# Macaron layer on one core: attention operands transposed by DMA, context normalised on three engines, steps reordered

## What is computed

```python
x = x + 0.5 * ffn(layernorm(x))
x = x + attention(layernorm(x))
x = x + 0.5 * ffn(layernorm(x))
# ffn: W = base + mean|w - base| * sign(w - base); (silu(x W1') * (x W3')) W2', inner width 1792
# attention: 32 query heads of 16, 8 key/value heads (4 queries each), rotary embedding,
# scores / 16, causal mask over 1024 tokens, softmax, context, dense projection with bias
```

## Time and profile before

| | |
|---|---|
| median of three runs | 1528.28 us |
| the profiled execution, its own time | 1528.74 us |
| its span, first to last instruction | 1527.0 us |
| busy: TensorE, VectorE, ScalarE, GpSimd | 1452.4, 869.9, 646.4, 158.5 us |
| granted TensorE clock, mean | 0.98 |
| last projection matmul ends | 572.2 us |
| last parts_k written (L1273), wd_raw load issued (L393) | 579.33, 579.36 us |
| first score matmul of attention | 581.54 us |
| four context transpositions (L1751), start of the first to end of the last | 0.63 to 0.66 us |

### The profile page before, as it was taken

One profiled execution on the slowest core, in us unless ns is written; L12 is line 12 of the kernel. 1 busy time (PEld: TensorE's weight loads), 2 busy tenths in 40 slices (PEclk: granted clock), 3 DMA queues, 4 the chain that ended last, 5 costly groups with the idle time before them and its releaser, 6 DMA issues.

```text
span 1527.0 us, 25186 instructions
## 1 busy us (share of the span) xinstructions
PE 1452.4 (95%) x9648; PEld 650.4 (43%) x9648; DVE 869.9 (57%) x1362; ACT 646.4 (42%) x900; POOL 158.5 (10%) x235
## 2 busy tenths in 40 slices
PE   1999999999999995999999999999999999999998
PEld 0444444444444452343434343334444444444443
DVE  7998414414453767899999999955412412412212
ACT  5863112212222454688888888763212112112111
POOL 1000000000000441223232222210000000000000
PEclk9999999999999995799999999999999999999999
DMA  9605500000000001000000000024000000000000
GB/s 387 221 0 192 232 0 1 0 0 1 1 1 1 1 1 35 2 2 2 2 23 10 3 2 3 2 97 193 1 0 0 29 0 0 28 0 1 28 0 27
DMA packets 17035, 58.42 MB, mean 38 GB/s; under 512 B 4912, under 2 KB 4912, under 8 KB 16432
## 3 DMA queue, kind: packets, MB, share of 16 engines
q1 hardware_dynamic: 16944, 57.15, 9.7%
HBM read 40.63 MB, written 15.20 MB: 37 GB/s over the span
## 4 chain that ended last, share of the span: by engine, by line
PE 92%; DVE 4%; issue 1%; ACT 1%; DMA 1%; POOL 0%; SPq 0%; DVEq 0%; ACTq 0%; POOLq 0%
PE ps L1482 38%; PE ps L1503 17%; PE ps L1741 10%; PE ps L1656 7%; PE ps L1722 5%; PE ps L1643 4%; PE ps L1845 3%; PE ps L1529 2%; PE ps L1476 1%; PE ps L1751 1%; DVE rowmax L1310 1%; PE ps L1615 1%; PE ps L1660 1%; DMA w_raw<-w1t 1%; PE ps L1618 1%
## 5 line engine op out<-in xcount | busy, mean ns | idle before, releaser
L778 ACT ACTIVATE probs<-ps 128x1024 f32<-128x1024 f32 (+3 forms) x384 | 296.1, 814 | 64.6 <-PE ps L1722 61.5
L1482 PE MATMUL ps<-xt_hi,w_all 128*128 128x512 f16 x896 | 275.9, 381 | 9.3 <-DVE w_all L989 9.3
L1310 DVE TENSOR_REDUCE rowmax<-ps 128x2 f32<-128x1024 f32 (+3 forms) x208 | 237.1, 1140 | 15.8 <-PE ps L1664 7.3
L1144 DVE SCALAR_TENSOR_TENSOR hb<-ps,scal,silub 128x512 f32<-128x512 f32 x56 | 42.0, 750 | 267.4 <-PE ps L1482 267.4
L1656 PE MATMUL ps<-ka,qa 48*128 48x512 f16 (+3 forms) x768 | 165.8, 346 | 16.4 <-DVE rowmax L1310 10.1
L1482 PE MATMUL ps<-xt_lo,w_all 128*128 128x512 f16 x448 | 170.8, 381 | 0.0
L1741 PE MATMUL ps<-probs,vs 128*32 128x512 f32 (+3 forms) x1536 | 164.4, 500 | 0.0
L1314 DVE TENSOR_REDUCE rowmax<-ps 128x1 f32<-128x512 f32 x192 | 131.1, 683 | 16.9 <-PE ps L1656 14.0
L1482 PEld LDWEIGHTS ps<-xt_hi,w_all 128*128 128x128 f16 (+1 forms) x896 | 87.9, 98 | 115.4 <-issue 11.7
L1722 PE MATMUL ps<-qa,ka 50*128 50x512 f16 (+3 forms) x768 | 134.5, 330 | 0.1
L1503 PE MATMUL ps<-w32b_all,hhib 128*128 (+1 forms) x448 | 133.4, 379 | 0.0
(11 more groups left out here) (169 smaller groups left out, 2175.8 us busy)
## 6 DMA issues: line engine op xcount, KB each, us to landing
spill<-w_all SPq DMA_DIRECT2D x1, 10752.0 KB, 28.9
w32b_all<-spill SPq DMA_DIRECT2D x1, 7168.0 KB, 20.4
x<-x_in SPq DMA_DIRECT2D x4, 1024.0 KB, 5.2
y_out<-x SPq DMA_DIRECT2D x4, 1024.0 KB, 4.2
wbase<-m1t SPq DMA_DIRECT2D x4, 896.0 KB, 12.6
w_raw<-w1t SPq DMA_DIRECT2D x4, 896.0 KB, 14.2
wbase<-m3t SPq DMA_DIRECT2D x4, 896.0 KB, 24.4
w_raw<-w3t SPq DMA_DIRECT2D x4, 896.0 KB, 24.3
```

Of the source, the lines that this page charges most:

```text
L778: nc.scalar.activation(probs[u % PBUF][:, 2 * pair:2 * pair + 2, 0:q1 - q0], wide(("scores", g, (u, pair)))[:, :, 0:q1 - q0], ACT.Exp, sca ...
L1144: nc.vector.scalar_tensor_tensor(out=bufs["h"][u][:, :], in0=ps[:, UP, :], scalar=scal[:, 1:2], in1=bufs["silu"][u][:, :], op0=ALU.mult, o ...
L1310: nc.vector.tensor_reduce(dst, src, AX.X, ALU.max).then_inc(pair_taken, 1)
L1482: last = mm(ps[:, bank, :], w[a][:, k, bass.ts(t, P)], xt[b][:, k, :], start=(k == 0 and n == 0), stop=(k == HB - 1 and n == 2))
```

## The change

A group g stays a batch and four query heads, but now two heads belong to kv head i (an even one) and two to i + 1: the host permutes the columns of the query weights and bias, and the rows of the dense weights, accordingly (head_order). One key operand, with key i on partitions 0 to 63 and i + 1 on 64 to 127, serves two groups. The 32 transpositions, three PSUM bank uses and three ScalarE copies a group are gone, and SP issues DMA transpositions from parts to qa and ka instead, 8 a group for qa and 8 every second group for ka, three groups ahead. The places 48 to 63 of parts_q and parts_k are filled by GpSimd. The context goes from PSUM to SBUF by a ScalarE copy (take_turned), VectorE inverts the sums from there, and GpSimd makes the product. The order of pieces, scores, values and all engines' steps in the loop and the tail is another one.

```diff
+    def placed(g):
+        return 16 * SEQ_TILES * (2 - g % 2) * (g // BUF + 1)
...
@@ SP
+        def place_operands(g):
+            b, i = divmod(g, KV_HEADS)
+            for tt in range(SEQ_TILES):
+                sp.dma_start_transpose(qa[g % BUF][:, :, tt * P:(tt + 1) * P],
+                                       parts_q[:, SEQ_TILES * b + tt, Q_PER_KV * i:Q_PER_KV * (i + 1), :].rearrange("p h c -> p (h c)"))\
+                    .then_inc(qk_placed[g % BUF], 16)
+                if g % 2 == 0:
+                    sp.dma_start_transpose(ka[g // 2 % BUF][:, tt * P:(tt + 1) * P].unsqueeze(1),
+                                           parts_k[:, SEQ_TILES * b + tt, i:i + 2, :].rearrange("p h c -> p (h c)"))\
+                        .then_inc(qk_placed[g % BUF], 16)
+        sp.wait_ge(qklo_ready, 2 * SEQ_TILES)
+        sp.wait_ge(qkhi_ready, 2 * SEQ_TILES)
+        sp.wait_ge(kpad_ready, 4 + SEQ_TILES)
+        sp.wait_ge(lnt_full, 8 * TPC)
+        place_operands(0)
+        place_operands(1)
+        sp.wait_ge(qkv_full, 12)
+        place_operands(2)
         sp.wait_ge(qklo_ready, 2 * TOKEN_TILES)
         sp.wait_ge(v_ready, TOKEN_TILES)
         sp.dma_start(wd_raw[:, :, :], wdt.rearrange("(t p) n -> p t n", p=P)).then_inc(wd_loaded, 16)
...
+        place_operands(3)
         for g in range(GROUPS):
             sp.wait_ge(wide_taken, drained(("rowmax", g, 0)))
...
+            if 1 <= g < GROUPS - 3:
+                sp.wait_ge(st_full, 2 * NU * g)
+                place_operands(g + 3)
@@ GpSimd
+            nc.gpsimd.memset(parts_q[:, i, :, ROWS:64], 0.0).then_inc(kpad_ready, 1)
...
+        def normalise(g, c):
+            pool.wait_ge(rec_ready, g * 2 + c + 1)
+            nc.gpsimd.tensor_tensor(out=dst, in0=ctx_row[:, :, :, 0:HEAD],
+                                    in1=rec[:, :, :].unsqueeze(3).to_broadcast([P, 4, Q_PER_KV, HEAD]),
+                                    op=ALU.mult).then_inc(row_normal, 1)
         for k in range(GROUPS + 2):
+            mask_unit(k - 2, 5)
+            mask_unit(k - 2, 6)
             mask_unit(k - 2, 7)
             mask_unit(k - 2, 8)
+            normalise(k - 2, 0)
...
             mask_unit(k - 1, 3)
-            mask_unit(k - 1, 5)
-            mask_unit(k - 1, 6)
+            normalise(k - 2, 1)
@@ ScalarE
+        def take_turned(g, c):
+            act.wait_ge(ctxt_full, g * 2 + c + 1)
+            if c or g:
+                act.wait_ge(row_normal, g * 2 + c)
+            nc.scalar.copy(ctx_row[:, :, :, :], t[:, :, :, 0:HEAD + 1]).then_inc(single_taken, 1)
@@ VectorE
-            nc.vector.reciprocal(rec[:, :, :], t[:, :, :, HEAD]).then_inc(rec_ready, 1)
-            nc.vector.tensor_tensor(out=dst, in0=t[:, :, :, 0:HEAD],
-                                    in1=rec[:, :, :].unsqueeze(3).to_broadcast([P, 4, Q_PER_KV, HEAD]),
-                                    op=ALU.mult).then_inc(single_taken, 1)
+        def invert_sums(g, c):
+            dve.wait_ge(single_taken, taken(("ctx", g, c)))
+            if c or g:
+                dve.wait_ge(row_normal, g * 2 + c)
+            nc.vector.reciprocal(rec[:, :, :], ctx_row[:, :, :, HEAD]).then_inc(rec_ready, 1)
...
             reduce_piece(k, 10)
+            invert_sums(k - 2, 0)
             reduce_piece(k, 11)
...
             split_rowmax(k)
+            invert_sums(k - 2, 1)
@@ TensorE
-        def transpose_qk(g, o):
...
-        pe.wait_ge(raw_ready, TOKEN_TILES)
-        for o in range(3):
-            transpose_qk(0, o)
         for k in range(GROUPS):
...
             if r == 0:
-                pe.wait_ge(wide_taken, drained(("qk", k, 2)))
+                pe.wait_ge(qk_placed[k % BUF], placed(k))
...
                 pe.wait_ge(m_placed, 64 * g + 64)
+                if g == 0:
+                    pe.wait_ge(raw_ready, TOKEN_TILES)
...
-                last = mm(ps[32 * h:32 * h + 32, CTX_BANK, at:512], vs[g % BUF][:, kt, :],
+                last = mm(ps[32 * h:32 * h + 32, CTX_BANK, at:512], vs[g // 2 * 2 % BUF + h % 2][:, kt, :],
```

More of the change, by code:

```diff
@@ L279, in build @@
     vs_ready = sem("vs_ready")
-    qkt_full = sem("qkt_full")
+    qk_placed = [sem(f"qk_placed{i}") for i in range(BUF)]
+    row_normal = sem("row_normal")
     pair_full, single_full = sem("pair_full"), sem("single_full")
@@ L410, in _ @@
         sp.wait_ge(spilled, 16)
-        sp.wait_ge(wide_taken, drained(("qk", GROUPS - 1, 2)))
+        sp.wait_ge(m_placed, 64 * GROUPS)
+        for v in range(BUF):
+            sp.wait_ge(qk_placed[v], placed(GROUPS - BUF + v))
         sp.dma_start(w1b_all[:, :], spill.ap()[:, 0:W_T]).then_inc(w1_back, 16)
@@ L726, in _ @@
         ffn(0, ffn1)
-        def take_qk(g, o):
-            if g >= GROUPS:
-                return
-            act.wait_ge(qkt_full, 3 * g + o + 1)
-            dst = qa[g % BUF][:, o, :] if o < 2 else ka[g % BUF][:, :]
-            nc.scalar.copy(dst, wide(("qk", g, o))[:, 0, :].bitcast(F16)).then_inc(wide_taken, 1)
         def high_parts(i):
@@ L1419, in _ @@
         norm_rows(8, 0)
+        invert_sums(14, 0)
         context_high(2)
@@ L1444, in _ @@
         context_low(6)
+        invert_sums(15, 0)
         add_dense(5)
@@ L1599, in wide_free @@
                 pe.wait_ge(wide_taken, WIDE[use] - 1)
-        def transpose_qk(g, o):
-            if g >= GROUPS:
-                return
-            b, kv = divmod(g, KV_HEADS)
-            if o == 0:
-                pe.wait_ge(qkhi_ready, 2 * SEQ_TILES * (b + 1))
-                pe.wait_ge(qklo_ready, 2 * SEQ_TILES * (b + 1))
-                pe.wait_ge(kpad_ready, 4)
-            wide_free(("qk", g, o))
-            bank = wide(("qk", g, o))[:, 0, :].bitcast(F16)
-            for tt in range(SEQ_TILES):
-                if o < 2:
-                    h = Q_PER_KV * kv + 2 * o
-                    src = parts_q[:, SEQ_TILES * b + tt, h:h + 2, :].rearrange("p h c -> p (h c)")
-                    last = tr(bank[:, tt * P:(tt + 1) * P], src, ident16[:, :])
-                else:
-                    for at_row in (0, 64):
-                        last = tr(bank[at_row:at_row + 64, tt * P:(tt + 1) * P], parts_k[:, SEQ_TILES * b + tt, kv, :],
-                                  ident16[:, :])
-            last.then_inc(qkt_full, 1)
         def qkv(i):
@@ L1681, in score_piece @@
                     for b in (0, 1):
-                        last = partial(PAIR_BANK + b, off, b, v, qt, j, k0, w)
+                        last = partial(PAIR_BANK + b, off, b, k, qt, j, k0, w)
                     off += w
@@ L1693, in score_piece @@
             for qt, slot, j, k0, w in parts:
-                last = partial(SINGLE_BANK, off, kind, v, qt, j, k0, w)
+                last = partial(SINGLE_BANK, off, kind, k, qt, j, k0, w)
                 if k0 + w == P * (qt + 1):
@@ L1752, in transpose_context @@
             last.then_inc(ctxt_full, 1)
-        pe.wait_ge(raw_ready, TOKEN_TILES)
-        for o in range(3):
-            transpose_qk(0, o)
         for k in range(GROUPS):
+            scores_t(k - 2, 5, 0)
+            score_piece(k, 0)
+            values(k - 2, 2)
+            values(k - 2, 3)
+            score_piece(k, 1)
+            scores_t(k - 2, 5, 1)
+            score_piece(k, 2)
+            scores_t(k - 2, 6, 0)
+            score_piece(k, 3)
+            values(k - 2, 4)
+            score_piece(k, 4)
@@ L1848, in project @@
                 last.then_inc(dense_full, 1)
+        scores_t(14, 5, 0)
+        values(14, 2)
+        values(14, 3)
+        scores_t(14, 5, 1)
+        scores_t(14, 6, 0)
+        transpose_rows(0)
+        values(14, 4)
+        scores_t(14, 6, 1)
         scores_t(14, 7, 0)
+        project(0, 0)
+        project(0, 1)
         values(14, 5)
         scores_t(14, 7, 1)
+        transpose_rows(1)
         scores_t(14, 8, 0)
-        transpose_rows(0)
-        scores_t(14, 8, 1)
+        project(0, 2)
```

299 lines of the change are left out of this document (142 added, 157 removed).

## The result

The changed kernel takes 1538.62 us (median of 4 runs, 1535.84 to 1541.77), the kernel before 1527.94 (4 runs, 1527.18 to 1528.32): a ratio of 1.0063, 95% interval 1.0051 to 1.0076. Slower, where 1506.5 was forecast.

The account below looks back on a forecast made before the run. TensorE was taken to bound the loop and tail, VectorE close behind in the loop. Gains 2.8 + 1.3 + 2.5 + 18.2 - 3.0 = 21.8 from 1528.74 gave 1506.9, forecast as a median of 1506.5 us, range 1495 to 1525.

Parts of the forecast that it names:

- SP's queue, "Cost zero, hidden by that room": SP's issue of 16 transpositions a burst, 0.6 to 1.0 us each, fits a room of 20.1 us in a turn.
- the break-even at 1.5: Time per transposition on SP's queue at which bursts of 16 would cancel the 21.8 us gain: 1.5 us each.
- the late operands: Rival, chance 0.17: transpositions over 1.5 us each on SP's queue; at 2.0, 71 us lost in bursts, about 1578.
- The new turn, 24.3: Attention loop: 23.7 plus old idle 0.2 plus 0.4 of new waits; turns 2 to 15 gain 14 x 1.3 = 18.2 us.
- TensorE's floor of 23.7: Loop turn: TensorE's 25.4 us less 1.7 for the removed transpositions.
- VectorE's floor of 22.4: Loop turn: VectorE's floor falls from 23.2 to about 22.4 us as normalisation work leaves it.
- the lockstep rival: Loop, chance 0.15: VectorE's idle stays, so a turn shrinks only by VectorE's relief, 0.9 us; 1512.
- "up to 0.5" for the new wait on ScalarE's copy: End of VectorE's turn: the second inverse waits for ScalarE's copy and the next maxima queue behind it; up to 0.5 us.
- Start 2.8 and turn 0 1.3: First scores run at 572, saving VectorE's 2.85 us wait (2.8); turn 0 loses transposition waits of 0.71 and 0.57 (1.3).
- Turn 1, 2.5: Turn 1 gains 2.5 us: no parts_k wait of 1.38, fewer transposition steps, five units of scores and values instead of seven.
- Tail, -3.0: Score and value units moved from turn 1 to the tail at full clock, 3.3 us by columns; -3.0 with overlap.
- the flat rival: Loop, chance 0.05: the order recovers nothing, as in turn 15; about 1524.5, 1525 to 1531 with a third of a mask wait.

Follow-up runs that it names:

- a1_load_first: The changed kernel with group 2's 16 transpositions behind the loads of the dense weight and its bias on SP's queue; 1526.79 us.
- b1_even: a1_load_first with the keys of a pair of groups placed in two halves, at most 12 transpositions a group in the loop; 1517.37 us, 0.9934 of before.
- b2_product_dve: b1_even with the two products a turn of context by inverse moved from GpSimd to VectorE; 1529.8 us, turns of 25.73.
- a3_old_order: The kernel before, in its old order, without the TensorE transpositions and ScalarE copies of groups 4 to 15; 1529.38 us, turns 25.51.
- d1_less_pe: b1_even with value products of units 1 and 2 of each group cut from 384 and 256 columns to 64; 1514.64 us, turns 24.39.
- e1_warm_22: b1_even, second inverse one maximum later, plus extra unread 128-row products: 34 behind piece 1, 2 behind each later piece of turn 0 and each of turn 1; 1512.42 us.
- a4_one_dma: The changed kernel with, from group 4 on, one 2048-column transposition for eight query ones and one of 1024 for eight key ones; 1531.72 us.
- c4_warm_2: b1_even, second inverse one maximum later, plus extra unread 48-row products: 34 behind piece 1, more behind turn 0's later pieces, none in turn 1; 1530.2 us.
- d2_warm_rows: c4_warm_2 with extra products over 128 rows: 34 behind piece 1, 3 behind each later piece of turn 0, 1 behind each of turn 1; 1515.71 us.
- c3_less_pe: b1_even with six of the eight value products of unit 1 of each group left out; 1518.42 us, turns of 24.67.
- a2_no_late_keys: The changed kernel without the key transpositions of groups 8, 10, 12 and 14, whose scores use older keys; 1530.41 us.

## Why the prediction was wrong

**SP's queue, "Cost zero, hidden by that room".** This step failed. It took 0.6 to 1.0 us for a transposition from the issue of qa<-mrow; the trace shows 1.28 from start to start. By the prediction's own arithmetic 16 x 1.28 = 20.5 is already over its room of 20.1, and the measured burst is 21.2. It also put the break-even at 1.5 by pricing the bursts alone, and so took transpositions over 1.5 us apart as the sign of being wrong: that sign did not come, the other one, score matmuls that wait for qa<-mrow, did (six times, 7.3 us). The sentence beside it, that 40 transpositions at over 0.9 each hold wd_raw back and dense_scale with it, was exact in mechanism (53.4 us for 40, 1.33 each; 595.71 against 579.36) and had no price in the rival. It was worth 9.0 us (a1_load_first). The bursts and the weight copies were worth 9.9 in the whole (1526.79 to 1516.87, the profiled run of b1_even), which is 11.0 in turns 2 to 15 less 1.1 for a projection that ended later. Without both the changed kernel is a faster one. So the late operands, given 0.17, are the rival that came: at 1.28 us each and not at 2.0, with some 10 us from the bursts and not 71, and with 9 us from a place that its sum left out.

The Trainium skill (DMA: Bandwidth & Descriptors, "Anatomy of one DMA") gives about 2.0 us fixed per DMA, for those that GpSimd issues; these are issued by SP, and land 2.4 us after their issue. Paid one after another, as that sentence of the prediction had it, 2.0 us would have made a burst 32 us; the trace shows 21.2, spaced by the issue.

**The new turn, 24.3.** Too low: undisturbed 24.69. TensorE's floor of 23.7 was about right (busy 23.93), and nothing here shows VectorE's floor of 22.4 to be wrong. The step that failed is to start from TensorE's floor alone and add 0.6 of waits: the turn did not follow TensorE's relief. From a single maximum to what follows VectorE mostly takes 0.65 to 0.8, and not 0.60, because it waits shortly for TensorE again and again. VectorE's own relief and no more came through, which was the lockstep rival (0.9 a turn, given 0.15): b2_product_dve shows it from one side, a3_old_order from the other. That TensorE's work counts in part in the new order is shown by d1_less_pe, and goes beyond that rival. The "up to 0.5" for the new wait on ScalarE's copy was right (0.36), and moving it gave 0.27 a turn.

**Start 2.8 and turn 0 1.3.** Right for the start: the first scores run at 571.7, and VectorE goes from its last parts_k straight on to the first maximum (2.85 us of waiting gone, 578.79 in b1_even). Turn 0 is shorter by 0.8 instead of 1.3, from its first maximum to its split (27.39 against 28.20). That b1_even ends it 4.2 us before the kernel before (606.18 against 610.38), with 4.1 forecast, is in part luck: 0.5 of it is a projection that ended earlier in that run. In the changed kernel as it is, the late weight hid the gain.

**Turn 1, 2.5.** Wrong: 28.67 in b1_even against 28.18. The prediction let the low clock "last a little into turn 2"; in fact it fills turn 1 of b1_even to 632, 26 of its 28.67 us, where in the kernel before it ended at 629 of a turn that went on to 638.56. At a clock of 0.93 the turn is 25.88 (e1_warm_22, with the inverse moved), 2.3 less than before: near the forecast gain, for a clock that was not there. In the changed kernel as it is, the slow split behind the late weight comes on top (30.27). Why before's clock came back earlier was not tested; it had more for TensorE in that turn (24.97 busy against 20.43).

**Tail, -3.0.** Measured -4.6. The mechanism is right, the size was too small. TensorE by line in b1_even from 980.26 on:

```profile
L1770 PE MATMUL ps<-probs,vs 128*32 128x512 f32 (+3 forms) x176 | 17.9, 491 | 0.0
L1751 PE MATMUL ps<-qa,ka 50*128 50x512 f16 (+3 forms) x76 | 12.6, 336 | 0.7 <-ACT probs L824 0.7
```

Before, from 996.78 on, it was 15.1 (144 matmuls) and 11.2 (66). Scores grew by 1.4 us, as in the sum; values by 2.8 instead of 1.9, by 32 matmuls or four units instead of three, since before one unit of the tail had run ahead of VectorE's split. The tail's window is 4.25 us longer (86.74 against 82.49), TensorE's busy time 3.7 of it and its idle time 0.6, where it now waits 0.7 us for ScalarE's exponentials. The other 0.4 lie behind the tail, in the second feed-forward step, and have no cause here.

Summed for b1_even, in spans: 4.2 - 0.5 + 12.8 - 4.6 = 11.9, from 1527.0 to 1515.1. The forecast had 21.8: 5.4 too much for turns 2 to 15, 3.0 for turn 1, 1.6 for the tail. The rest of the miss, 19.0 us between the profiled runs of after and b1_even, is SP's queue.

One figure of the flat rival does not follow: a third of a mask wait of 0.67 in 14 turns adds 3.1 us to 1524.5, which gives 1527.6; how it comes to 1531 is not said.

## What to carry to other kernels

An edit that moves work to DMA moves it to the issuing queue as well: multiply the number of instructions by the time that one takes to issue, and if no row has that kind of instruction, let a price from below and above decide the sign before it is called hidden. Then list everything that stands behind them in that queue, each with its own due time; here one weight load behind 40 small transpositions cost as much as all the bursts. Between two engines in lockstep, test which one's work the turn follows: here taking 6% of its work from the fuller one bought nothing in the old order, and 3% bought 0.30 of 24.69 us in the new one, while the work given to the other cost its full length.

## What was not expected of the hardware

- SP is held 1.25 us by a transposition of 256 columns and 1.23 by one of 128, but only 1.9 and 1.8 in the median by one of 2048 and of 1024 (a4_one_dma); a plain copy takes 0.59. The Trainium skill (Advanced Engine Details and Errata, "X-Bar Transpose (TRN2)") says that transposing DMAs are as fast as regular ones; in the time of issue of small ones the trace disagrees by a factor of two (1.25 against 0.59).
- The granted clock fell to 0.50 at about 580 with TensorE busy 6.00 of 6.00 us on 48-row products, and stayed at 1.00 there with the same number of 128-row products (c4_warm_2, d2_warm_rows).
- Six of the eight value products of a unit left out, those of three of the four heads that lie side by side on 32 columns each, did not lower TensorE's busy time (23.92 against 23.93, c3_less_pe).
- VectorE's three instructions of the split took 2.4 to 2.6 us instead of 0.6 where GpSimd's work on the weight ran beside them (after, a2_no_late_keys, a4_one_dma), and 0.6 where it did not (a1_load_first, b1_even).
